# Mixer: the next step's products one slot earlier, the turning of y and the ranks earlier on TensorE, the expert tile's bank read after both rows of exponentials, the softplus after small parts

## What is computed

```python
x = x + attn(layernorm(x))          # x: 8 x 512 tokens x 512
x = x + ffn(layernorm(x))

# attn: in_proj -> x, z (1024 each); short causal convolution over 4 tokens, silu
x_dbl = xc @ x_proj_w.T             # 128 for dt, 16 for B, 16 for C
delta = softplus(dt_r @ dt_proj_w.T + dt_proj_bias)
h = h * exp(delta * A) + (delta * x_t) * B_t     # per channel, 16 states, token by token
y = (h * C_t).sum(states) + xc * D_param
out = (y * silu(z)) @ out_proj_w.T

# ffn: softmax router over 8 experts, the best 2, their weights made to sum to 1
h = silu(rows @ w1[e]) * (rows @ w3[e]);  out = h @ w2[e]    # 512 -> 1792 -> 512
```

## Time and profile before

| | |
|---|---|
| median of 3 runs | 4637.71 us (4635.84 to 4641.01) |
| the profiled execution, its own time | 4637.9 us |
| its span, first to last instruction | 4636.1 us |
| VectorE busy over the whole span | 2411.8 us (52%) |
| TensorE busy over the whole span | 4149.5 us (90%) |
| mixer, to the last small parts of its router | about the first 2554 us |
| experts | the rest |

### The profile page before, as it was taken

How to read it: one execution, slowest core, us unless ns; L and a number is a source line. 1 busy time by engine, 2 the same in 40 slices (tenths; PEclk the granted TensorE clock), 3 DMA queues, 4 the chain that set the end, 5 groups by cost and what they waited for, 6 DMA issues and landing times. The chain is left out here.

```text
span 4636.1 us, 70329 instructions
## 1 busy us (share of the span) xinstructions
PE 4149.5 (90%) x25764; PEld 3362.7 (73%) x25764; DVE 2411.8 (52%) x3197; ACT 1932.2 (42%) x4080; POOL 1835.0 (40%) x1416
## 2 busy tenths in 40 slices
PE   5777888888888888888877599999999999999999
PEld 4555667766776777667755588888888888888887
DVE  2999998998998989989987100000000000000000
ACT  5767777777777767777764000000000000000000
POOL 2767768766786687667755000000000000000000
PEclk8788999999999999999988799999999999999999
DMA  3022353545354435443533303031030303021300
GB/s 132 30 76 96 112 164 111 168 146 164 111 163 151 163 107 164 154 160 112 162 118 98 134 14 109 14 104 20 16 109 14 109 14 109 14 87 35 108 16 14
DMA packets 289343, 451.99 MB, mean 97 GB/s; under 512 B 15862, under 2 KB 183414, under 8 KB 280822
## 3 DMA queue, kind: packets, MB, share of 16 engines
q1 hardware_dynamic: 273078, 412.71, 27.1%
q0 software_dynamic: 14768, 34.41, 4.0%
q10 hardware_dynamic: 1296, 2.37, 0.1%
HBM read 920.96 MB, written 45.95 MB: 209 GB/s over the span
## 5 line engine op out<-in xcount | busy, mean ns | idle before, releaser
L546 POOL TENSOR_TENSOR hs<-hs,bc 128x1024 f32<-128x1024 f32 x512 | 1213.5, 2370 | 340.2 <-DVE hs L1114 317.7
L1114 DVE TENSOR_TENSOR_SCAN hs<-dA,pU 128x1024 f32<-128x1024 f32 x512 | 1168.8, 2283 | 53.1 <-ACT dA L651 31.2
L1562 ACT ACTIVATE gate<-pA 128x512 f32<-128x512 f32 x216 | 117.5, 544 | 1859.8 <-PE pB L1604 1859.8
L651 ACT ACTIVATE dA<-delta,aneg 128x255 f32<-128x255 f32 x2048 | 854.2, 510 | 28.5 <-DVE hs L1114 21.9
L1477 POOL DMA_INDIRECT out<-ow,trow x54 | 83.5, 1547 | 1971.5 <-DVE ow L1699 1971.5
L1604 PE MATMUL pA<-xT,w1s 128*128 128x128 f32 x6048 | 799.8, 275 | 0.7 <-ACT xT L1575 0.7
L1604 PE MATMUL pB<-xT,w3s 128*128 128x128 f32 x6048 | 799.7, 275 | 0.0
L970 PE MATMUL pY<-ident,hs 128*128 128x128 f32 x4096 | 569.0, 288 | 238.8 <-POOL hs L546 238.4
L1604 PEld LDWEIGHTS pA<-xT,w1s 128*128 128x128 f32 x6048 | 741.1, 192 | 26.4 <-issue 25.4
L970 PEld LDWEIGHTS pY<-ident,hs 128*128 128x128 f32 x4096 | 492.9, 148 | 341.4 <-issue 170.7
L1604 PEld LDWEIGHTS pB<-xT,w3s 128*128 128x128 f32 x6048 | 736.9, 192 | 0.0
(11 more groups left out here) (203 smaller groups left out, 3480.5 us busy)
## 6 DMA issues: line engine op xcount, KB each, us to landing
w1s<-in_w SPq DMA_DIRECT2D x165, 1024.0 KB
w3s<-in_w SPq DMA_DIRECT2D x165, 1024.0 KB
w2s<-in_w SPq DMA_DIRECT2D x165, 1024.0 KB
ew<-in_w SPq DMA_DIRECT2D x273, 512.0 KB, 4.3
win<-in_w_in SPq DMA_DIRECT2D x128, 512.0 KB, 3.9
bc<-bc_d SPq DMA_DIRECT2D x64, 1024.0 KB, 10.6
w1s<-in_w SPq DMA_DIRECT2D x55, 512.0 KB
w3s<-in_w SPq DMA_DIRECT2D x55, 512.0 KB
```

Of the source, the lines that this page charges most:

```text
L546: pool.tensor_tensor(hs[b][:, :, :], hs[b][:, :, :], bc[:, N + g * PN:N + (g + 1) * PN, :], ALU.mult)\
L651: e = act.activation(dA[k % NB][:, i, 1:T], delta[:, c, 1:T], ACT.Exp, scale=aneg[:, c, n:n + 1])
L1114: dve.tensor_tensor_scan(hs[b][:, :, :].rearrange("p n t -> p (n t)"), dA[b][:, :, :].rearrange("p n t -> p (n t)"), pU[:, :, :].rearrange ...
L1562: act.activation(gate[q % 2][:, 0:n, :], pA[q % 2][:, 0:n, :], ACT.Silu).then_inc(silu, 1)
```

## The change

It is a change of order, with the same operations in the mixer; `experts` is untouched. By part:

- TensorE and ScalarE: `bc` goes from slot 9 to 8, `dtr` from 10 to 9, `dt(0)` to `dt(3)` with their `read_dt` from slots 11 and 12 to 10 and 11. The z products go from slots 13, 14, 15 and the next step's slot 0 to slots 12 to 15.
- The second layernorm's turned rows are made one block of 128 at a time: the first in slot 10 after the up-product, the second in slot 11. The logits move behind `dt(3)`.
- TensorE: `turn_y` stands before the second `sums` of its slot; the ranks stand before the z product and the down-products of slot 14. The down-products are dealt 3, 4, 3, 4 to slots 12 to 15 where it was 4, 3, 3, 4.
- ScalarE: the reading of the expert's bank (`empty`) stands behind both rows of exponentials, at the head of `beside`; `copy_y` comes before the rest; the square root of slot 7 comes before the silu; the square root for the first layernorm goes from slot 14 to 13.
- GpSimd: `multiply` comes one piece later.
- VectorE: `finish` comes one piece later (g == 2), parts of the first layernorm a little earlier, and the small parts at the step's end stand before the softplus.
- SyncE: `bc_d` is stored before the expert loads 11 to 13.

```diff
-        UP0, DOWN = 4, {12: (0, 4), 13: (4, 7), 14: (7, 10), 15: (10, 14)}
+        UP0, DOWN = 4, {12: (0, 3), 13: (3, 7), 14: (7, 10), 15: (10, 14)}
...
@@ gpsimd
-                    if early(s)[0] and i % PPU == 1 and UP0 + 1 <= i // PPU <= UP0 + ROUNDS:
-                        multiply(s - EARLY0, i // PPU - UP0 - 1)
+                    if early(s)[0] and i % PPU == 0 and UP0 + 2 <= i // PPU <= UP0 + ROUNDS + 1:
+                        multiply(s - EARLY0, i // PPU - UP0 - 2)
@@ scalar
                 def halfway(u):
-                    q = u - UP0 - 1
-                    if tile and 0 <= q < ROUNDS:
...
-                    if u in (11, 12) and front:
-                        read_dt(2 * (u - 11))
+                    if u in (10, 11) and front:
+                        read_dt(2 * (u - 10))
+                    if u == 10 and back:
+
+                        ge(act, scale2, r + 1)
+                        ge(act, x1_stored, 16 * r + 16)
+                        for t in range(TT):
+                            act.activation(xb[:, t, 0:D], xb[:, t, 0:D], ACT.Identity, bias=nb[1][:, t:t + 1],
+                                           scale=rs[1][:, t:t + 1]).then_inc(xn2, 1)
+                    if u == 11 and back:
+                        copy_x2(1)
...
+                def empty(u):
+                    q = u - UP0 - 1
+                    if tile and 0 <= q < ROUNDS:
+                        ge(act, ew_used, EWLOADS * jt + 2 * q + 2)
+                        ge(act, e_h, ROUNDS * jt + q)
+                        act.activation(eth[:, :, :], pEup[:, 0, :, :], ACT.Tanh, scale=0.5).then_inc(e_half, 1)
+                        act.activation(eab[:, :, :, :], pEup[:, :, :, :], ACT.Copy).then_inc(e_out, 1)
...
                 def beside(u):
-                    rest(u)
+                    empty(u)
                     if u == 0 and back:
                         copy_y(r, CH - 1)
                     if scan and u % UPC == 0 and u > 0:
                         copy_y(s, u // UPC - 1)
+                    rest(u)
...
-                    if u in (11, 12) and front:
-                        read_dt(2 * (u - 11) + 1)
+                    if u in (10, 11) and front:
+                        read_dt(2 * (u - 10) + 1)
                     if u == 10 and back:
...
+                        copy_x2(0)
-                    if 13 <= u <= 15 and front:
-                        copy_z(u - 13, f, szf)
+                    if 12 <= u <= 15 and front:
+                        copy_z(u - 12, f, szf)
@@ tensor
-                    if u == 9 and front:
+                    if u == 8 and front:
                         ge(pe, xc_ready, f + 1)
...
-                    if u == 10 and front:
+                    if u == 9 and front:
                         ge(pe, bc_copied, f + 1)
...
+                    if u in (10, 11) and front:
+                        dt(2 * (u - 10))
                     if u == 11 and back:
+                        turn_x2(1)
                     if u == 14 and back:
...
                         m.then_inc(rank_mm, 1)
+                    if 12 <= u <= 15 and front:
+                        z_pair(u - 12, f, xnT[1 - odd])
+                    if tile:
+                        expert(u)
...
                     if tile:
                         expert_up(u)
-                    if u in (11, 12) and front:
-                        dt(2 * (u - 11) + 1)
+                    if u in (10, 11) and front:
+                        dt(2 * (u - 10) + 1)
+                    if u == 10 and back:
+                        turn_x2(0)
+                    if u == 11 and back:
...
+                        m.then_inc(logits_mm, 1)
+                    if scan and u % UPC == 0 and u > 0:
+                        turn_y(s, u // UPC - 1, odd)
                     if scan:
                         sums(u, 1)
...
-                    if scan and u % UPC == 0 and u > 0:
-                        turn_y(s, u // UPC - 1, odd)
@@ vector
-                    if scan and u % UPC == 0 and c >= 2 and g == 0:
+                    if scan and u % UPC == 0 and c >= 2 and g == 2:
                         finish(s, c - 2, odd)
...
-                if picks:
-                    pick(0)
+                if back:
+                    place(3)
                 if ln1_too:
                     ln1(s + 2, 8)
                 if picks:
-                    pick(1)
+                    for i in range(4):
+                        pick(i)
                 if front:
                     softplus(0)
```

More of the change, by code:

```diff
@@ L413, in step @@
                 if tile:
-                    for i in range(9, 14):
+                    for i in range(9, 11):
                         load_expert(i)
@@ L421, in step @@
                     sp.dma_start(bc_d, bcs[:, :]).then_inc(bc_stored, 16)
+                if tile:
+                    for i in range(11, 14):
+                        load_expert(i)
                 if tile:
@@ L690, in rest @@
                             i.then_inc(taps_in, 1)
+                    if u == 7 and back:
+                        ge(act, var2, r + 1)
+                        act.activation(tiny2[1][:, :], mv2[:, :, 1], ACT.Sqrt, bias=series[:, 2:3]).then_inc(sd2, 1)
                     if u == PAIRS + 3 and front:
@@ L698, in rest @@
                         act.activation(bcs[:, :], pM[0:2 * N, 0, :], ACT.Copy).then_inc(bc_copied, 1)
[L699 to L702 removed]
+                    if u == 9 and front:
                         ge(act, dtr_mm, f + 1)
                         act.activation(dtr[:, :], pM[:, 1, :], ACT.Copy).then_inc(dtr_copied, 1)
[L705 to L706 removed]
+                    if u in (10, 11) and front:
+                        read_dt(2 * (u - 10) + 1)
                     if u == 10 and back:
[L709 to L718, removed]
+                        copy_x2(0)
+                    if u == 11 and front:
                         ge(act, dt_read, 4 * f + 4)
@@ L843, in expert_up, with turn_x2 @@
                             m.then_inc(ew_used, 1)
+                def turn_x2(t):
+                    ge(pe, tcopied1, TT * (f + 1) if front else TT * STEPS)
+                    ge(pe, xn2, TT * r + t + 1)
+                    ge(pe, tcopied2, TT * r + t)
+                    for d in range(DC):
+                        m = pe.transpose(pT[:, d, :], xb[:, t, d * P:(d + 1) * P], ident[:, :])
+                    m.then_inc(turned2, 1)
                 def project(ps, rowsT, w, h):
@@ L980, in step @@
                         expert_up(u)
-                    if u in (11, 12) and front:
-                        dt(2 * (u - 11) + 1)
+                    if u in (10, 11) and front:
[3 more added lines that the diff above has]
+                    if u == 11 and back:
+                        ge(pe, tcopied2, TT * r + TT)
+                        ge(pe, x1_ready, TT * r + TT)
+                        for t in range(TT):
+                            for d in range(DC):
+                                m = pe.matmul(pR[:, 0, t, :], xnT[odd][:, d, t * P:(t + 1) * P], wgate[:, d, :],
+                                              start=d == 0, stop=d == DC - 1)
+                        m.then_inc(logits_mm, 1)
+                    if scan and u % UPC == 0 and u > 0:
+                        turn_y(s, u // UPC - 1, odd)
                     if scan:
```

60 lines of the change are left out of this document (15 added, 45 removed).

## The result

The changed kernel takes 4657.36 us, the median of 6 runs (4656.1 to 4662.02), against 4636.77 us (4633.98 to 4641.01) for the kernel before on the same chips: a ratio of 1.0044, 95% interval 1.0034 to 1.0055. It is slower by 20.6 us. The profiled execution took 4656.1 us, its span is 4654.4 us (before: 4637.9 and 4636.1).

What follows compares the result with a forecast made beforehand. VectorE was taken to pace the mixer, with 139.0 us of waits in steps 3 to 14 to win. Forecast: 4637.9 - 7.0 + 20.8 + 4.4 - 2.0 = 4654.1 us, range 4620 to 4680.

Steps and rivals of the forecast that it cites:

- Waits that go: VectorE, steps 3 to 14: waits for turned y (61.2 us), ranks (40.7) and square root (6.3) vanish.
- Scan 18: VectorE's wait before this scan grows from 2.11 to 3.6 us in even steps; none in odd steps.
- Scan 23: VectorE waits before this scan for late exponentials: 2.9 us in even steps, 1.0 us in odd.
- Logits: They stand behind dt(3), so VectorE's top(0) waits 2.0 us a step.
- Scan 24: Bank reading, last up-product, dt(1), read_dt(1) and exponentials in series, 9.2 us: VectorE waits 5.3 us, odd steps 5.2.
- TensorE's clock: After 4.7 us idle the last up-product runs partly at half clock: 1.73 us in 12 steps, 20.8 us.
- rival at full clock: Same series of waits before scan 24, but no slow last up-product: 4633.3 us, chance 0.27.
- The sum: New VectorE waits, 13.8 us even and 8.2 us odd, six steps each: 132.0 us against 139.0; clock charge 20.8.
- Parts at nothing: Before step 0: z product +4.4 us, square root -2.0; small parts before the softplus within 0.3 us a step.

Runs made afterwards that it cites:

- after_filled: Changed kernel with 28 more products of ident on TensorE, in its idle gap ahead of the last up-product: 4637.3 us, ratio 1.0000.
- after_bank_first: Changed kernel with the expert's bank read between the two rows of exponentials, ahead of read_dt(0), and multiply one piece earlier: 4576.64 us, ratio 0.9870.
- after_dt_behind: Changed kernel with read_dt(0) and the normalised rows behind slot 10's exponentials and the bank reading: 4576.14 us, ratio 0.9875.
- logits_filled: after_bank_first with VectorE's top calls later, plus 14 products of ident on TensorE ahead of its wait for dt(3): 4540.47 us, ratio 0.9800.
- before_turns: Kernel before with only turn_y ahead of the second sums, finish one piece later, and ranks ahead of slot 14's z product: 4622.65 us, ratio 0.9972.

## Why the prediction was right

The forecast was 4654.1 us, slower, from a chain of hand-offs and a fall of the clock; measured 4657.36. By its steps:

- **Waits that go.** 108.2 us forecast; none of them is left in the list. Right.
- **Scan 18.** 3.6 us forecast, 3.95 in the even step shown. **Scan 23.** 2.9 and 1.0 forecast; 2.63 and 1.52. (By the walk's own rows, 1373.60 + 0.95 + 19.2, the scan stands at 1393.75 and not 1393.6, which makes 2.75 of the 2.9.) **Logits.** 2.0 forecast; 2.11, and 2.2 on average. Each within about 0.5 us.
- **Scan 24.** The chain as forecast, link by link: the gap of TensorE 4.7 us forecast, 4.58 in the rows; the wait 5.3 us at full clock, 5.2 in odd steps, 63.0 in twelve; `after_filled` shows 5.35, 5.15 and 63.05. `after_bank_first` and `after_dt_behind` break it in two different places and both win 81 us, so the chain is shown and not only argued.
- **TensorE's clock.** Right in kind, undersized: I charged the last up-product 1.73 us, from one row at 0.68 behind a shorter gap. It costs 6.14 - 3.74 = 2.40 us on average, 28.8 us instead of 20.8. This is the main term that was mis-sized. The rival at full clock (4633.3 us) is, in effect, `after_filled`: 4637.3. What spoke for that rival was misread: the trace of the kernel before has six gaps of 1.17 to 1.19 us before an up-product in these steps, that before 1374.37 among them, and behind all six the up-product took 5.40 to 5.47 us.
- **The sum.** VectorE's waits for exponentials and logits are 169.0 us, forecast 132.0 + 20.8 = 152.8. The 16 us more, summed over all twelve steps, are scan 24 (90.6 against 63.0 + 20.8, so 6.8, all of it the clock, since it waits 63.05 with the gap filled), scans 18 and 23 (3.6 together), the logits (2.6), and 3.1 us at scans 0, 6 and 10, which the forecast leaves out.
- **Parts at nothing.** Two misses that went the other way. The small parts before the softplus were costed at nothing within 0.3 us a step; the 24 `uv` operations of steps 3 to 14 take 40.7 us against 49.3, 8.6 us less, by the block beside `weigh`. Before step 3 I forecast 2.4 us more and it was 3.4 less. The z product does stand on the path (3.81 us of ScalarE's wait for it, 88.65), and its 4.4 us were right: the kernels run here differ in how fast TensorE did the in-projection before all that moved, and of two executions alike in that, the one with the change's order starts step 0 later by 4.5 us (`logits_filled` 108.30 against 103.77 for the kernel before; `after_filled` 105.58 against 101.06 for `before_turns`). The changed kernel's traced execution was quick there; one in-projection before and after:

```profile
30.39 6.68 PE L848 MATMUL pM<-xnT,win 128*128 128x256 f32 x16 [3.17 <-issue]
```

```profile
29.33 3.69 PE L867 MATMUL pM<-xnT,win 128*128 128x256 f32 x16 [3.16 <-issue]
```

From 30 to 46 us the granted clock is 0.69 in the one and 0.95 in the other. This gave the changed kernel's traced execution 5.7 us (102.60 against the 108.30 of `logits_filled`) that its order has no part in; why the clock differs there was not followed.

In steps 3 to 14 the sum was +13.8 us and the trace says +22.9; at the start and the end +2.4 and it was -4.5. The errors offset each other, and that is luck: the total is closer (2.0 us on the profiled execution, 4656.1) than its terms. With the start of the kernel before it would have been about 7.7 us off, still inside the range. The sign and the place stand on their own: without the chain the same parts make the kernel 1.3% faster.

## What to carry over

When steps of two chains go into one engine's queue, write down for each what it waits for. Here ScalarE served `dt(0)`, then exponentials, then the bank, and two chains that had run side by side became one of 9 us; moving either of the two past the other gave 81 us back. An engine's idle gap just ahead of a step on the path may cost twice, as wait and as clock, and products without any use in the gap can pay (20 and 24 us here). And a part tried alone says little where several waits are nearly due: the turns alone gave 13 us, with the sooner products and the bank first the change gives 60.

## What the runs showed of the hardware

TensorE's last up-product took 5.44 to 6.73 us behind 4.58 us of idleness, 3.84 with 28 products ahead of the gap's last 1.53 us, and 3.74 without a gap in `after_bank_first`; the logits fell from 3.28 to 1.85 us when their gap was filled. What surprised me was that a gap of 2.25 us, filled but for 0.39 and 0.11 us of it, was worth 24 us: the slow stretch behind it also held the z product (4.66 us against 3.67). And a VectorE operation held up by GpSimd is counted as busy (a pair of 3.66 or 4.28 us, where each takes 1.23 alone): no wait in any list showed the 0.6 us a step that the small parts could use.
